# Three of eight low parts of each next expert's weights made by GpSimd instead of VectorE, in a decoder layer with a mixture of experts

## The chip, the cores and the metric

The kernel runs on one core of a Trainium2 chip. The metric is the device time of one execution in microseconds (us). Before the change three runs gave 993.51, 994.58 and 995.72 us, median 994.58.

## The reference

One decoder layer over 32 sequences of 128 tokens with 256 channels, all in fp32, with a layer norm after each of three parts:

```python
x = layernorm(x + retention(x, past_kv, W_qkv, gn_weight, gn_bias))     # 16 heads of 16
x = layernorm(x + cross_attention(x, ctx, Wq, Wk, Wv, Wo, bo))          # causal, 16 heads
x = layernorm(x + moe(x, router_w, w_fc, b_fc, w_proj, b_proj))

# moe: 4096 tokens, 8 experts, 256 -> 1024 -> 256, the two best experts of each token
probs = softmax(xf @ router_w.T); topk_probs, topk_idx = top_k(probs, 2)
combine = topk_probs / sum(topk_probs), scattered to [tokens, 8]
h = gelu_new(einsum('nc,ech->neh', xf, w_fc) + b_fc)
y = einsum('nec,ne->nc', einsum('neh,ehc->nec', h, w_proj) + b_proj, combine)
```

Only the third part is touched here. The kernel computes an expert only for the tokens that are sent to it.

## The kernel before, in words

The attention part runs sequence by sequence until about 540 us. While it runs, GpSimd (POOL) sends each token's row to a region of its two experts in device memory. From about 510 to 960 us come the experts (their first slot is mixed with the last sequences). The rows of an expert are worked off in slots of 256 rows. Four early slots of expert 0 come first, then `expert` runs for each of the eight experts over its own slots (a loop whose count is read from a table).

The matmuls need more than one pass of the reduced fp32 format (fp32r), so every operand is split into a high part (rounded to fp32r) and a low part (the original minus the high part). Within a slot there are eight steps j, one for each 128 of the 1024 hidden channels:

- PE (TensorE): `fc(j)`, six matmuls into a bank (line 820), and three steps later `proj(j-3)`, four matmuls (lines 834 and 836), which read the hidden values' high and low parts. In step 5 it also transposes the next slot's rows (line 801).
- ACT (ScalarE): `hidden` makes the high part of gelu (line 1155) and its full value `h_f` (line 1161). The second waits for the low part of two steps before (`h_split`), since `h_f` has two buffers. After step 7, `xs_high` makes the next slot's `xs_hi` (line 1148).
- DVE (VectorE): `hidden_low` subtracts, `h_lo = h_f - h_hi` (line 1490), which releases `proj(j)`. After j = 0 it weights the slot before (lines 1529, 1532), which releases POOL's scatter-adds. After j = 7 it makes `xs_lo` (line 1460), which lets PE start the next slot, and after that adds the biases (lines 1516, 1521).
- POOL (GpSimd): `add`, two indirect DMAs a slot that add the weighted rows to `residual_sum` (line 1714).

An expert's weights are loaded into `w_raw` by the SP queue and split into eight pieces of 128x512. This is done in the first slot of the expert before it, so in seven first slots: ACT makes the high parts 0 to 6 behind each `hidden` (`split_hi`, line 1075), DVE high part 7 (`last_hi`, line 1380), and DVE all low parts behind each `hidden_low` (`split_lo`, line 1385). Each low part waits for its high part (`raw_hi`) and counts in `w_ready`; after the last one DVE waits until all eight are counted, and then lets SP load new weights. Expert 0's own weights are split in the attention part, where POOL makes the low parts (`first_low`, line 1746).

All five queues run in written order, and are tied only by semaphores: an instruction that waits holds up all that stands behind it on its engine.

Of the kernel before, what the change touches and what calls it, by code (L numbers as in the profile page):

```python
# [16 lines left out]
HC = H // P  # L17
# [13 lines left out]
DRAIN_IDLE = 3  # L31
EARLY = 4
EARLY_SEQ = 27
MOST = 2 * N_TOK // SLOT + E + EARLY
BITS = 10 * P + 2 * TW
SMALL = 2 * P + 33
# [27 lines left out]
def decoder_kernel(nc, x, turned, kv_blocks, w_qkv, gn_scale, gn_shift, wq_t, wk_t, wv_t, wo_t, bo,  # L64
                   router_t, w_fc, b_fc, w_proj, b_proj, decay_c, small_c, bits_c, out):
    f32, f32r, bf16 = mybir.dt.float32, mybir.dt.float32r, mybir.dt.bfloat16
    i32, u32 = mybir.dt.int32, mybir.dt.uint32
    ALU, ACT, AX = mybir.AluOpType, mybir.ActivationFunctionType, mybir.AxisListType
# [3 lines left out]
    with ctx:  # L72
        def sb(name, shape, dt=f32):
            return ctx.enter_context(nc.sbuf_tensor(name, shape, dt))
# [7 lines left out]
        def sem(name):  # L82
            return ctx.enter_context(nc.semaphore(name))
# [20 lines left out]
        w_raw = sb("w_raw", [P, WROW])  # L104
# [132 lines left out]
        w_hi, w_lo = ([w[:, i, :] for w in w_both] for i in range(2))  # L237
# [46 lines left out]
        s = {k: sem(k) for k in names}  # L284
# [66 lines left out]
        def _(sp):  # L351
# [44 lines left out]
            def early_rows(g):  # L396

                if g:
                    sp.wait_ge(s["rows_turned"], g + EVER)
                    sp.wait_ge(s["meta_ready"], g + EVER)  # L400
                    apart(sp)
                sp.dma_start(rows[:, :, :],
                             sent_flat[g * SLOT:(g + 1) * SLOT, :].rearrange("(h p) c -> p h c", p=P))\
                    .then_inc(s_rows, 16)

            def step(k):
# [5 lines left out]
                if k == B - 1:  # L412
                    for r in range(4):
                        sp.wait_ge(s_sent[r], 32 * len(range(r, EARLY_SEQ, 4)))
                    early_rows(0)
# [57 lines left out]

            n_all = sp.value_load(tab_i[0:1, 3, 0:1], min_val=E + EARLY, max_val=MOST)
            sp.wait_ge(s["rows_turned"], n_all + EVER)
# [9 lines left out]
            out_rows = out.rearrange("b t c -> (b t) c")  # L485
            n_add = sp.value_load(tab_i[0:1, 3, 1:2], min_val=16 * (E + EARLY), max_val=16 * MOST)
            for half in range(HALVES):
# [471 lines left out]
        def _(act):  # L959
# [19 lines left out]
            def w_high(i):  # L979

                hi, _, raw, loaded, n = parts[i]
                act.wait_ge(s[loaded], n)
                A(hi, raw, ACT.Copy).then_inc(s["w_high"], 1)
# [258 lines left out]
        def _(dve):  # L1242
            V = nc.vector

            def w_low(i):

                hi, lo, raw, _, _ = parts[i]
                dve.wait_ge(s["w_high"], i + 1)
                V.tensor_tensor(lo, raw, hi.bitcast(f32), ALU.subtract).then_inc(s["w_split"], 1)
# [111 lines left out]
            def put(c):  # L1361
# [9 lines left out]
                dve.sem_inc(s["placed"], 1)  # L1371
                if c.n == EARLY_SEQ - 1:
                    V.tensor_scalar(filled[:, 0:1], filled[:, 0:1], float(EARLY * SLOT), None, ALU.max)

            PIECE = WROW // HC

            def last_hi(e, par):
                at = slice((HC - 1) * PIECE, HC * PIECE)
                dve.wait_ge(s["raw_hi"], HC * (e + 1) - 1)
                V.tensor_copy(w_hi[par][:, at], w_raw[:, at]).then_inc(s["raw_hi"], 1)  # L1380

            def split_lo(e, par, j):
                at = slice(j * PIECE, (j + 1) * PIECE)
                dve.wait_ge(s["raw_hi"], HC * e + j + 1)
                last = V.tensor_tensor(w_lo[par][:, at], w_raw[:, at], w_hi[par][:, at].bitcast(f32),
                                       ALU.subtract)
                last.then_inc(s["w_ready"], 1)
                if j == HC - 1:
                    dve.wait_ge(s["w_ready"], HC * (e + 1))
                    dve.sem_inc(s["raw_split"], 1)  # L1390
# [67 lines left out]
            def split_rows(g):  # L1458
                dve.wait_ge(s["xs_chain"], g + 1)
                V.tensor_tensor(xs_lo[:, :, :].rearrange("p k t -> p (k t)"), ps_xs(g)[:, :],  # L1460
                                xs_hi[:, :, :].bitcast(f32).rearrange("p k t -> p (k t)"), ALU.subtract)\
                    .then_inc(s["xs_ready"], 1)
# [22 lines left out]
            def hidden_low(g, j):  # L1485

                dve.wait_ge(s["h_done"], HC * g + j + 1 + EVER)
                if j >= 4:
                    dve.wait_ge(s["y_done"], HC * g + j - 3)
                V.tensor_tensor(h_lo[j % 4][:, :], h_f[j % 2][:, :], h_hi[j % 4][:, :].bitcast(f32),  # L1490
                                ALU.subtract).then_inc(s["h_split"], 1)

            def slot(g, e, split_to=None, beside=None):
                for j in range(HC):
                    hidden_low(g, j)
                    if j == 0:
                        gate_rows(g - 1)
                    if j == HC - 1:
                        split_rows(g + 1)
                    if split_to and j == HC - 1:  # L1500
                        last_hi(*split_to)
                    if split_to:
                        split_lo(*split_to, j)
                    if beside:
                        beside(j)
                add_rows(g, e)

            def add_rows(g, e):

                dve.wait_ge(s["meta_ready"], g + 1 + EVER)  # L1510
                V.tensor_copy(meta[:, :, :], meta_next[:, :, :]).then_inc(s["y_chain"], 1)
                dve.wait_ge(s["y_chain"], g + 1)
                take_rows(g + 1)
                dve.wait_ge(s["y_done"], HC * (g + 1))
                for half in range(HALVES):
                    V.tensor_tensor(y_b[:, half, :], ps_out(g, half), bproj(e), ALU.add)\
                        .then_inc(s["y_biased" if not two_sums(g) else "y_first"], 1)
                if two_sums(g):
                    for half in range(HALVES):
                        dve.wait_ge(s["y_first"], HALVES * (g - 2) + half + 1)  # L1520
                        V.tensor_tensor(y_b[:, half, :], ps_sum[half][:, C:2 * C], y_b[:, half, :], ALU.add)\
                            .then_inc(s["y_biased"], 1)

            def gate_rows(g):

                for half in range(HALVES):
                    dve.wait_ge(s_added[half], 16 * (g + EVER))
                    apart(dve)
                V.tensor_copy(meta_i[:, :], meta[:, :, 1])
                dve.wait_ge(s["y_biased"], HALVES * (g + 1) + EVER)  # L1530
                for half in range(HALVES):
                    V.tensor_scalar(y_w[:, half, :], y_b[:, half, :], meta[:, half, 0:1], None, ALU.mult)\  # L1532
                        .then_inc(s["y_weighted"], 1)
# [71 lines left out]
            dve.wait_ge(s["consts_expert"], 16 * CONSTS_EXPERT)  # L1605
            drain()
            slot(1, 0, None, last_norms)
            slot(2, 0, None, last_places)
            for g in range(3, EARLY - 1):
                slot(g, 0)  # L1610
# [44 lines left out]
        def _(pool):  # L1655
            G = nc.gpsimd
# [50 lines left out]
            def add(g, before):  # L1707
                for half in range(HALVES):

                    pool.wait_ge(s["y_weighted"], HALVES * g + half + 1)  # L1710
                    apart(pool)
                    pool.wait_ge(s_added[1 - half], 16 * (before + EVER))
                    apart(pool)
                    G.indirect_dma_start(total, bass.IndirectOffsetOnAxis(meta_i[:, half:half + 1], 0),  # L1714
                                         y_w[:, half, :], None, compute_op=ALU.add)\
                        .then_inc(s_added[half], 16)

            def drain():
# [8 lines left out]
                for r in range(4):  # L1727
                    pool.wait_ge(s_total[r], 16 * len(range(r, EARLY_SEQ, 4)))
                add(0, 0)
# [9 lines left out]

            PIECE = WROW // HC  # L1740

            def first_low(j):

                at = slice(j * PIECE, (j + 1) * PIECE)
                pool.wait_ge(s["raw_hi"], j + 1)
                G.tensor_tensor(w_lo[0][:, at], w_raw[:, at], w_hi[0][:, at].bitcast(f32), ALU.subtract)\
                    .then_inc(s["w_ready"], 1)
                if j == HC - 1:
                    pool.wait_ge(s["w_ready"], HC)
                    pool.sem_inc(s["raw_split"], 1)  # L1750
# [35 lines left out]
                pool.wait_ge(s_total[r], 16 * (B // 4))  # L1786

            def expert(e, par, n_slots, before, has_next, has_after):
                with pool.Fori(0, n_slots) as i:
                    add(before + i, before)  # L1790

# [91 lines left out]
```

## Time and profile before

| | |
|---|---|
| median of 3 runs | 994.58 us (993.51 to 995.72) |
| the profiled execution's own time | 990.76 us |
| its span | 988.7 us |
| mean granted TensorE clock | 0.978 |
| busy: PE, PEld (weight load), DVE, ACT, POOL | 924.2, 822.0, 664.0, 605.2, 385.0 us |
| low part of a piece on DVE, line 1385 | 56 times, mean 692 ns |
| `h_lo` on DVE, line 1490 | 288 times, mean 426 ns |
| scatter-add on POOL, line 1714 | 72 times, mean 1624 ns |

The profile is of one execution. Its own time lies 2.1 us over its span and 3.8 us under the median of the runs. Times in the timelines are microseconds from the start of the span. A duration in a row reaches from the start of an instruction to its last write, and the next one can begin before that: two subtractions of 128x512 and 128x256 on DVE overlap by 0.08 us. Line numbers are those of the kernel before.

### The profile page before, as it was taken

To read this page: it belongs to the slowest core of one execution; us is meant where nothing else is said; L and a number is where in the kernel's file an instruction comes from. 1 tells how busy PE (TensorE), PEld (TensorE's weight loads), DVE (VectorE), ACT (ScalarE), POOL (GpSimd) and SP (SyncE) were. 2 spreads that over 40 slices of the span, in tenths; PEclk is the share of its full clock that TensorE was granted. 3 is DMA by queue.
4 is the path that set the end of the run, shared out by engine and by line. 5 is a ranking of instruction groups with operands and counts; after the bars stand their busy time and mean duration, and the time that the engine had idled before them with its cause. 6 is when DMAs were issued, how large, how long until landed. Compare 5 with 4: busy or idle time off the path is not lost.

```text
span 988.7 us, 29856 instructions
## 1 busy us (share of the span) xinstructions
PE 924.2 (93%) x10845; PEld 822.0 (83%) x10845; DVE 664.0 (67%) x1977; ACT 605.2 (61%) x1528; POOL 385.0 (39%) x639
## 2 busy tenths in 40 slices
PE   5899999999999999999888999999999999999950
PEld 4788888888888888888667899999999999999950
DVE  3577777777877877877734677575755775665536
ACT  4556656656556666666446567565755765665536
POOL 0324555555544656664523522222222323232223
PEclk9999999999999999999989999999999999999985
DMA  8111141112111111122112453523435343533228
GB/s 279 50 34 56 61 142 45 56 55 66 56 49 45 62 56 61 55 64 85 44 30 44 119 130 58 138 44 53 129 53 139 79 103 53 129 48 46 45 37 336
DMA packets 57362, 79.91 MB, mean 81 GB/s; under 512 B 5728, under 2 KB 46048, under 8 KB 57120
## 3 DMA queue, kind: packets, MB, share of 16 engines
q1 hardware_dynamic: 41504, 58.50, 18.5%
q0 software_dynamic: 13536, 18.16, 10.8%
q10 hardware_dynamic: 2208, 1.73, 0.6%
q8 instruction: 71, 1.16, 0.5%
q14 instruction: 43, 0.35, 0.1%
HBM read 52.10 MB, written 29.71 MB: 83 GB/s over the span
## 4 chain that ended last, share of the span: by engine, by line
PE 79%; ACT 6%; DVE 5%; issue 4%; DMA 2%; SPq 1%; POOL 1%; ACTq 0%; DVEq 0%; POOLq 0%
PE bank L820 16%; PE bank L834 11%; PE bank L511 11%; PE bank L836 5%; PE bank L647 4%; PE bank L673 4%; PE bank L718 3%; PE bank L573 3%; PE bank L626 3%; PE bank L694 3%; PE bank L598 3%; PE bank L593 2%; ACT h_f L1161 2%; PE bank L732 2%; ACT last_out L1237 1%
## 5 line engine op out<-in xcount | busy, mean ns | idle before, releaser
L820 PE MATMUL bank<-xs_hi,w_both 128*128 128x256 f32 x1152 | 241.6, 287 | 0.0
L1155 ACT ACTIVATE h_parts<-bank,bfc_s 128x256 fp32r<-128x256 f32 x288 | 140.0, 486 | 155.3 <-PE bank L820 150.6
L1714 POOL DMA_INDIRECT residual_sum<-y_w,meta_i x72 | 116.9, 1624 | 300.4 <-DVE y_w L1532 267.0
L1490 DVE TENSOR_TENSOR h_parts<-h_f,h_parts 128x256 fp32r<-128x256 f32 x288 | 121.5, 426 | 143.9 <-ACT h_f L1161 138.4
L834 PE MATMUL bank<-w_both,h_parts 128*128 128x512 f32 x544 | 200.0, 398 | 1.1 <-DVE h_parts L1490 1.1
L820 PEld LDWEIGHTS bank<-xs_hi,w_both 128*128 128x128 f32 x1152 | 191.0, 190 | 7.8 <-issue 1.7
L820 PE MATMUL bank<-xs_lo,w_both 128*128 128x256 f32 x576 | 162.7, 282 | 0.0
L836 PE MATMUL bank<-w_both,h_parts 128*128 128x256 f32 x544 | 153.0, 281 | 0.0
L1161 ACT ACTIVATE h_f<-bank,bfc_s 128x256 f32<-128x256 f32 x288 | 139.4, 484 | 3.9 <-DVE h_parts L1490 3.4
L834 PEld LDWEIGHTS bank<-w_both,h_parts 128*128 128x128 f32 x544 | 102.5, 188 | 19.9 <-DVE h_parts L1490 3.5
L820 PEld LDWEIGHTS bank<-xs_lo,w_both 128*128 128x128 f32 x576 | 109.4, 190 | 0.1
L836 PEld LDWEIGHTS bank<-w_both,h_parts 128*128 128x128 f32 x544 | 102.7, 189 | 0.0
L1267 DVE TENSOR_REDUCE row_max<-bank 128x4 f32<-128x512 f32 x128 | 79.4, 682 | 6.9 <-PE bank L651 6.9
L1262 DVE TENSOR_TENSOR ret_p<-bank,decay 128x512 f32<-128x512 f32 x128 | 79.3, 682 | 1.6 <-PE bank L573 1.6
L1049 ACT ACTIVATE att_p<-bank 128x512 f32<-128x512 f32 x128 | 66.1, 603 | 22.0 <-PE bank L682 21.9
L1704 POOL DMA_INDIRECT sent_rows<-x_row,pos x64 | 64.2, 1003 | 22.2 <-issue 14.5
L673 PE MATMUL bank<-qx_own,kxT 32*128 32x256 f32 x512 | 45.0, 405 | 0.0
L647 PE MATMUL bank<-kxT,qx_own 32*128 32x128 f32 x1024 | 44.9, 287 | 0.0
L511 PE MATMUL bank<-h_parts,wqk_hi 128*128 128x256 f32 x128 | 39.2, 306 | 4.7 <-DVE xc_lo L1254 4.0
L647 PEld LDWEIGHTS bank<-kxT,qx_own 32*128 32x128 f32 x1024 | 36.2, 185 | 5.9 <-issue 3.0
L511 PE MATMUL bank<-wv_hi,h_parts 128*128 128x256 f32 x128 | 38.8, 303 | 2.2 <-ACT q_own L1001 2.0
L1013 ACT ACTIVATE v_ret<-bank 128x256 f32<-128x256 f32 x32 | 12.3, 384 | 46.5 <-PE bank L511 46.5
(184 smaller groups left out, 2139.7 us busy)
## 6 DMA issues: line engine op xcount, KB each, us to landing
rows<-sent_rows SPq DMA_DIRECT2D x37, 258.0 KB
xc_raw<-in_turned SPq DMA_DIRECT2D x32, 256.0 KB, 3.0
w_raw<-in_w_fc SPq DMA_DIRECT2D x8, 1024.0 KB
w_raw<-in_w_proj SPq DMA_DIRECT2D x8, 1024.0 KB
x_t<-in_x SPq DMA_DIRECT2D x32, 128.0 KB, 2.2
residual_sum<-x_row SPq DMA_DIRECT2D x32, 128.0 KB, 1.7
last_in<-residual_sum SPq DMA_DIRECT2D x7, 512.0 KB, 7.3
result<-last_out SPq DMA_DIRECT2D x7, 512.0 KB, 2.7
```

Of the source, the lines that this page charges most:

```text
L511: last = mm(to, left, right, start=(n == 0), stop=(n == len(passes) - 1))
L647: mm(ps_s[r][:, at], qx_own[c.r % 2][tile(r), k, j, :], kxT[c.n // 2 % 2][tile(r), k, c.n % 2 * T:(c.n % 2 + 1) * T], start=(k == 0 and j ...
L673: mm(ps_s[r][:, at], kxT[c.n // 2 % 2][tile(r), k, c.n % 2 * T:(c.n % 2 + 1) * T], qx_own[c.r % 2][tile(r), k, :, :].rearrange("p j t -> p ...
L820: last = mm(ps_h(g, j), w[:, at:at + P], v[:, k, :], start=(n == 0), stop=(n == 3 * NCH - 1))
L834: mm(ps_sum[half][:, :], h_hi[j % 4][:, cols], w[:, :, at:at + C], start=(j == 0), stop=False)
L836: last = mm(to, h_lo[j % 4][:, cols], w[:, 0, at:at + C], start=False, stop=(j == HC - 1))
L1155: A(h_hi[j % 4][:, :], ps_h(g, j), ACT.Gelu_apprx_tanh, bias=bias)
L1161: A(h_f[j % 2][:, :], ps_h(g, j), ACT.Gelu_apprx_tanh, bias=bias)\
L1262: V.tensor_tensor(ret_p[:, r, :], ps_s[r][:, :], decay[:, r, :], ALU.mult)\
L1267: V.reduce_max(row_max[:, r, 0:HPT], ps_s[r][:, :].rearrange("p (h s) -> p h s", s=T), AX.X)\
L1490: V.tensor_tensor(h_lo[j % 4][:, :], h_f[j % 2][:, :], h_hi[j % 4][:, :].bitcast(f32), ALU.subtract).then_inc(s["h_split"], 1)
L1714: G.indirect_dma_start(total, bass.IndirectOffsetOnAxis(meta_i[:, half:half + 1], 0), y_w[:, half, :], None, compute_op=ALU.add)\
```

## The change

In every first slot that has a next expert, the low parts 0, 1 and 2 of the next expert's weights are taken out of DVE's order and put into POOL's, ahead of the loop of scatter-adds of the present expert. The operands, the semaphores and their counts stay the same. POOL's scatter-adds of the last slot of the expert before still stand in front of the three low parts, since they belong to that expert's loop.

```diff
+ON_POOL = (0, 1, 2)
...
@@ vector, slot()
-                    if split_to:
+                    if split_to and j not in ON_POOL:
                         split_lo(*split_to, j)
...
@@ gpsimd
+            def split_lo(e, par, j):
+
+                at = slice(j * PIECE, (j + 1) * PIECE)
+                pool.wait_ge(s["raw_hi"], HC * e + j + 1)
+                G.tensor_tensor(w_lo[par][:, at], w_raw[:, at], w_hi[par][:, at].bitcast(f32), ALU.subtract)\
+                    .then_inc(s["w_ready"], 1)
...
             def expert(e, par, n_slots, before, has_next, has_after):
+                if has_next:
+                    for j in ON_POOL:
+                        split_lo(e + 1, 1 - par, j)
                 with pool.Fori(0, n_slots) as i:
                     add(before + i, before)
```

POOL's queue before, from the scatter-adds of one expert's loop to those of the next (`w_both` holds a weight piece's high and low parts; the branches are the loop's):

```order
L1714 DMA residual_sum<-y_w,meta_i 4352x256
L1710 REGISTER_ALU
L1714 DMA residual_sum<-y_w,meta_i 4352x256
L1789 REGISTER_ALU
L1789 COMPARE_AND_BRANCH
L1789 UNCONDITIONAL_BRANCH
L1789 ISA
L1712 ISA
L1714 DMA residual_sum<-y_w,meta_i 4352x256
```

The same place after the change (line numbers are 1 to 11 higher):

```order
L1715 DMA residual_sum<-y_w,meta_i 4352x256
L1711 REGISTER_ALU
L1715 DMA residual_sum<-y_w,meta_i 4352x256
L1800 REGISTER_ALU
L1800 COMPARE_AND_BRANCH
L1747 TENSOR_TENSOR w_both<-w_raw,w_both 128x512 x3
L1800 UNCONDITIONAL_BRANCH
L1800 ISA
L1713 ISA
L1715 DMA residual_sum<-y_w,meta_i 4352x256
```

Three subtractions now stand between the last pair of one expert and the first pair of the next.

DVE's queue before, steps 1 to 3 of a first slot (`h_parts` is the hidden values' high and low parts):

```order
L1532 TENSOR_SCALAR y_w<-y_b,meta 128x256 x2
L1385 TENSOR_TENSOR w_both<-w_raw,w_both 128x512
L1487 REGISTER_ALU
L1490 TENSOR_TENSOR h_parts<-h_f,h_parts 128x256
L1385 TENSOR_TENSOR w_both<-w_raw,w_both 128x512
L1487 REGISTER_ALU
L1490 TENSOR_TENSOR h_parts<-h_f,h_parts 128x256
L1385 TENSOR_TENSOR w_both<-w_raw,w_both 128x512
L1487 REGISTER_ALU
L1490 TENSOR_TENSOR h_parts<-h_f,h_parts 128x256
L1385 TENSOR_TENSOR w_both<-w_raw,w_both 128x512
```

And after:

```order
L1533 TENSOR_SCALAR y_w<-y_b,meta 128x256 x2
L1488 REGISTER_ALU
L1491 TENSOR_TENSOR h_parts<-h_f,h_parts 128x256
L1488 REGISTER_ALU
L1491 TENSOR_TENSOR h_parts<-h_f,h_parts 128x256
L1488 REGISTER_ALU
L1491 TENSOR_TENSOR h_parts<-h_f,h_parts 128x256
L1386 TENSOR_TENSOR w_both<-w_raw,w_both 128x512
```

Steps 3 to 7 of DVE, and the queues of PE, ACT and SP, keep their order.

## Rows read from the trace of the kernel before

**Rows 1.** The page, part 1: busy us of each engine, share, instructions.
```profile
PE 924.2 (93%) x10845; PEld 822.0 (83%) x10845; DVE 664.0 (67%) x1977; ACT 605.2 (61%) x1528; POOL 385.0 (39%) x639
```

**Rows 2.** Stretches: length, busy PE, PEld, DVE, ACT, POOL, granted clock, DMA.
```profile
597.45:608.00 10.55, 10.55 (x74) 9.58 (x74) 9.71 (x21) 9.34 (x23) 3.28 (x2) 1.00 0.30 43
610.00:622.00 12.00, 11.83 (x84) 10.90 (x83) 6.76 (x21) 6.85 (x17) 3.10 (x2) 1.00 0.33 55
```

**Rows 3.** Waits from 560 to 960 us: waiter, releaser, total us, times, longest.
```profile
DVE h_parts L1490 <- ACT h_f L1161: 124.6, 155, 1.7
...
PEld bank L834 <- DVE h_parts L1490: 3.5, 11, 0.4
...
PEld bank L820 <- issue: 1.3, 7, 0.2
```

**Rows 4.** Timeline, PEld, second expert: start, us, engine, line, [idle before].
```profile
606.82 0.19 PEld L834 LDWEIGHTS bank<-w_both,h_parts 128*128 128x128 f32 x1
...
607.64 0.19 PEld L820 LDWEIGHTS bank<-xs_hi,w_both 128*128 128x128 f32 x1 [0.18 <-issue]
...
610.94 0.19 PEld L834 LDWEIGHTS bank<-w_both,h_parts 128*128 128x128 f32 x1 [0.37 <-DVE h_parts L1490]
```

**Rows 5.** Timeline, ACT, first slot of the second expert.
```profile
597.45 0.63 ACT L1075 ACTIVATE w_both<-w_raw 128x512 fp32r<-128x512 f32 x1
...
598.68 0.65 ACT L1075 ACTIVATE w_both<-w_raw 128x512 fp32r<-128x512 f32 x1
...
605.74 0.57 ACT L1161 ACTIVATE h_f<-bank,bfc_s 128x256 f32<-128x256 f32 x1
```

**Rows 6.** Timeline, DVE, beginning of the same slot.
```profile
598.59 0.68 DVE L1385 TENSOR_TENSOR w_both<-w_raw,w_both 128x512 fp32r<-128x512 f32 x1
599.19 0.42 DVE L1490 TENSOR_TENSOR h_parts<-h_f,h_parts 128x256 fp32r<-128x256 f32 x1
599.53 0.68 DVE L1385 TENSOR_TENSOR w_both<-w_raw,w_both 128x512 fp32r<-128x512 f32 x1
```

**Rows 7.** Timeline, DVE, its second half.
```profile
603.11 0.69 DVE L1385 TENSOR_TENSOR w_both<-w_raw,w_both 128x512 fp32r<-128x512 f32 x1
...
606.34 0.43 DVE L1490 TENSOR_TENSOR h_parts<-h_f,h_parts 128x256 fp32r<-128x256 f32 x1
...
607.43 0.42 DVE L1380 CAST w_both<-w_raw 128x512 fp32r<-128x512 f32 x1
...
608.73 0.17 DVE L1511 COPY meta<-meta_next 128x4 f32<-128x4 f32 x1 [0.16 <-DVE w_both L1385]
```

**Rows 8.** Timeline, POOL, the same slot.
```profile
599.29 1.73 POOL L1714 DMA_INDIRECT residual_sum<-y_w,meta_i  x1 [7.94 <-DVE y_w L1532]
601.33 1.55 POOL L1714 DMA_INDIRECT residual_sum<-y_w,meta_i  x1 [0.31 <-issue]
```

**Rows 9.** Line 1746, POOL: count, ns min/median/max, first and last start.
```profile
L1746 POOL TENSOR_TENSOR w_both<-w_raw,w_both x8: 1278/1284/1287, 330.6 to 435.0; 128x512 fp32r<-128x512 f32 x8
```

**Rows 10.** Timeline, POOL, one of these low parts.
```profile
344.97 1.28 POOL L1746 TENSOR_TENSOR w_both<-w_raw,w_both 128x512 fp32r<-128x512 f32 x1
```

**Rows 11.** Timeline, DVE, beside it.
```profile
343.57 1.88 DVE L1262 TENSOR_TENSOR ret_p<-bank,decay 128x512 f32<-128x512 f32 x3
345.37 1.45 DVE L1254 TENSOR_TENSOR xc_lo<-xc_raw,h_parts 128x512 fp32r<-128x512 f32 x1
```

**Rows 12.** Line 1254, DVE: count, ns min/median/max.
```profile
L1254 DVE TENSOR_TENSOR xc_lo<-xc_raw,h_parts x32: 680/684/1452, 8.4 to 452.5; 128x512 fp32r<-128x512 f32 x32
```

**Rows 13.** Timeline, POOL, two small operations.
```profile
556.00 0.28 POOL L1682 TENSOR_TENSOR x_row<-gap_e,x_row 128x1 f32<-128x1 f32 x1
556.24 0.38 POOL L1683 TENSOR_TENSOR x_row<-tok,small 128x1 f32<-128x1 f32 x1
```

**Rows 14.** Timeline, DVE, beside them.
```profile
555.81 0.76 DVE L1490 TENSOR_TENSOR h_parts<-h_f,h_parts 128x256 fp32r<-128x256 f32 x2
```

**Rows 15.** A stretch with a PE gap of 2.80 us, columns as in rows 2.
```profile
524.00:530.00 6.00, 3.38 (x50) 3.07 (x52) 2.96 (x13) 5.08 (x9) 3.21 (x9) 1.00 0.30 82
```

## The prediction

> **What bounds the kernel now.** I read the busy times first, then stretches of the expert part, then the waits, and last the timelines of one first slot. PE is the bound: 924.2 of 988.7 us [rows 1]. The 10.55 us of a first slot are all PE, and so are 11.83 of 12.00 us in the slot behind it, at full clock; DVE and ACT are also near full in the first slot (9.71 and 9.34 us) and have room in the second (6.76 and 6.85) [rows 2]. Seven slots are such first slots, so the reader should ask what little PE loses there. In the whole expert part PE's weight loads wait 3.5 us for `h_lo` in 11 places and 1.3 us in 7 places for the next slot's `xs_lo` (shown as "issue") [rows 3]. The second expert shows where: no wait at the last `proj` at 606.82, 0.18 us at the first `fc` of the next slot, 0.37 us at its first `proj` [rows 4]. So the slack is used up at the end of a first slot: what is late there for `h_lo` of step 7 comes out of PE one for one.
>
> Who makes it late? ACT's period in the first slot is 1.23 us a step (597.45 to 598.68, two gelus and a high part) [rows 5]. DVE's work of a step is 0.60 + 0.34 = 0.94 us (598.59 to 599.19 for the low part, then to 599.53 for `h_lo`) [rows 6]. At step 7 ACT's `h_f` starts at 605.74 and lasts 0.57, to 606.31 [rows 5], and DVE's `h_lo` starts at 606.34 [rows 7]. DVE goes at ACT's pace there; it does not hold PE.
>
> **The change, part by part.** *Removed:* 3 low parts in 7 slots, 21 x 0.60 = 12.6 us of DVE's order. They lie in steps 0 to 2, at 598.59 to about 601 [rows 6]. Nothing behind them gets earlier at the slot's end, because from step 2 on DVE follows ACT again, and PE's waits stand behind step 7 [rows 4]. I value the removal at 0. All waits of [rows 3] on `h_lo` and `xs_lo` together, 4.8 us, would be its upper bound; its lower bound is 0, as less work in order can't delay DVE by itself.
>
> *Added:* 21 low parts on POOL at 1.284 us each [rows 9], 27 us. POOL has the time: its engine is busy 385.0 us [rows 1]. They stand behind the scatter-adds of the last slot of the expert before. That pair starts at 599.29, when DVE has weighted the rows, and ends at 601.33 + 1.55 = 602.88; the first add is long, 1.73 against 1.55, and may shorten to that when DVE's low parts beside it are gone [rows 8]. With 0.31 us between queue entries, as between the two adds, POOL's first low part can start at 599.29 + 1.55 + 0.31 + 1.55 + 0.31 = 603.0. All its high parts are long made. So the lows run in steps 4 to 7, the part in which PE's slack runs out, not in steps 0 to 2 from which they were taken.
>
> *What they meet there.* The trace has four low parts of POOL that a DVE subtraction with both operands in SBUF fell on. At 344.97 POOL begins, for 1.28 us [rows 10]; at 345.37 DVE begins `xc_lo`, of the same size, and takes 1.45 us instead of 0.684 [rows 11, 12]. It ends at 346.82, 0.57 behind POOL's end at 346.25. The pattern stands four times in the trace, with 1.44 or 1.45 us each, at the four of the eight low parts that met such a subtraction. The `ret_p` products beside the same low part, one of whose operands is a PSUM bank, keep their pace: 1.88 us for three [rows 11]. So DVE's two-SBUF-operand instructions stand still until POOL is done reading; DVE loses 346.82 - 0.684 - 344.97 = 1.17 us from POOL's start. The other way round, POOL's small operations at 556.00 and 556.24 stretch while DVE makes two `h_lo` back to back, and the first of them finishes between the two [rows 13, 14]: the two engines take turns.
>
> The Trainium skill states the same ("SBUF — State Buffer", Who interferes with whom): a VectorE instruction with two SBUF inputs and a GpSimd instruction that reads SBUF exclude each other, and the later one waits for the whole instruction of the first. By that rule a low part holds DVE 1.28 us, by the rows 1.17 us. The trace agrees with the rule but for this 0.11 us, and its consequence speaks against the change; the sum below takes both as ends.
>
> *The sum in one first slot.* `h_lo` (h_f and h_parts) and `split_lo` (w_raw and w_both) both read twice from SBUF. From 603.0 until `h_lo` of step 7, the shared access has to carry POOL's three low parts, 3 x 1.17 = 3.51 to 3 x 1.28 = 3.84 us, and DVE's low 4, h5, low 5, h6, low 6: 3 x 0.60 + 2 x 0.34 = 2.48 us. `h_lo` of step 7 then starts at 603.0 + 2.48 + 3.51 = 608.99 to 609.32, not 606.34 [rows 7]: 2.65 to 2.98 us late. Whether POOL comes first, the turns alternate, or POOL goes three times in a row, the sum of the work is the same. ACT's step 7 waits for `h_lo` 5, but that is done by about 607 in each order, before it matters. PE's slack at that point is 0, so PE loses the same. Behind it the tail (`xs_lo`, high part 7, low part 7, biases) is DVE's as before, with POOL finished, and the 0.37 us wait of the next slot stays. I take 2.85 us, nearer to the end that adds a handover.
>
> *Total:* 7 x 2.85 = 20.0 us. On the profiled execution, 990.76 + 20.0 = 1010.8. That execution lies 3.8 us under the median of the runs; on the median, 994.58 + 20.0 = 1014.6. The ends 2.65 and 2.98 give 1013.1 to 1015.4. If the adds stay long, POOL starts about 0.2 to 1 us later, which costs up to 0.3 us more a slot: 1017.5.
>
> *No cost:* the longer way of `w_ready`: POOL's last low part ends near 608.7, before DVE's own low part 7, which moves from before 608.73 [rows 7] to past 611. The new load of weights starts later by the same 2.85 us as the slot that needs it. The next scatter-add comes a slot later. PE's gaps: in the stretch with a gap of 2.80 us the granted clock stayed 1.00 [rows 15], so I charge nothing for a fallen clock, though mine are as long.
>
> **The rivals.**
> *DVE keeps the access while it has a backlog.* POOL's first low part delays low 4 by 603.0 + 1.17 - 603.11 = 1.06 us; DVE then runs low 4, h5, low 5, h6, low 6 in 2.48 us and starts step 7 at 606.65, 0.3 late. POOL's second and third fall in the tail: high part 7, a copy at 607.43, may wait too, and the wait for `w_ready` becomes the bound, with POOL's last part ending at about 606.65 + 0.34 + 2 x 1.28 = 609.6 and DVE's `meta` copy at 609.8 instead of 608.73 [rows 7]. That is 1.1 to 1.5 us a slot, 7 x 1.3 = 9.1: 1003.7. For it: back-to-back instructions may keep hold of it. Against: the small POOL operation that got in between two `h_lo` [rows 13, 14].
>
> *No exclusion that counts, so no slower.* The mechanism would be that POOL works its low parts beside DVE at 1.28 us each. They are done by 603.0 + 3.84 = 606.8, 2 us before `w_ready` is wanted; PE loses nothing, and DVE's lag at step 1 is gone. Gain 0 to 1 us: 993.6 to 994.6. It decides if the delay of a DVE low part beside POOL's is under some 0.1 us. Against it stand four delays of 0.76 us; for it only that those are `xc_lo`, and no expert slot has shown it.
>
> *More than counted:* the clock falls in the gaps. At the half level each microsecond of PE work takes one more; if two microseconds of work behind each gap ran so, 7 x 2 = 14 us more, 1029. For it: several gaps close behind one another; against: [rows 15].
>
> **How the numbers follow.** Exclusion with turns 0.68, a backlog that keeps DVE going (or something between the two) 0.21, no exclusion that counts 0.06, more than counted 0.05. The predicted time is that of the first, 1014.6. The low end goes to the second case, 1002.5, the high end to 1019.5 for long adds and dearer handovers; what is left out is the third and fourth case and the edges. A measurement can tell about 0.2% (2 us) from no change. The third case splits into 0.02 faster and 0.04 same; the others are all slower, with 0.94.
>
> **What would show it.** Right: three subtractions of about 1.3 us on POOL in each first slot, starting 5.5 us behind the first high part; beside them `h_lo` and `split_lo` of up to 1.6 us; a wait of PE for `h_lo` of 2 to 3 us at the end of each first slot; seven of these, and every other slot as before. Wrong: `h_lo` of 0.43 us beside POOL's low parts; or POOL's low parts themselves stretched to 3 us with PE's wait moved behind `meta` (the second case); or low parts that start before step 3.

## The result, and the profile after

The changed kernel took 1018.61 us (median of 4 runs, 1014.83 to 1020.75) against 995.02 us for the kernel before (4 runs). The two medians differ by 23.6 us. The ratio is 1.025 with a 95% interval of 1.0228 to 1.0272, so 2.5% slower: 24.8 us of the 993 us that the kernel before took in the later runs (medians 992.96 to 993.85). The forecast was 20.0 us slower, with a range up to 1019.5 us. The median lies just inside it; 1.025 times the 995.02 us of the kernel before gives 1019.9 us and lies just outside. The sign and the exclusion of DVE by POOL held. The size was short by a fifth, DVE and POOL took no turns, and PE waited mostly in the middle of the slot, not at its end.

The page of the profile after, busy times as in [rows 1], and three groups of part 5 (line, engine, operation, busy time, mean ns, idle time before and what ended it). Line numbers on DVE and PE are one higher than before:

```profile
PE 938.9 (92%) x10845; PEld 832.5 (82%) x10845; DVE 678.6 (67%) x1956; ACT 605.3 (59%) x1528; POOL 405.9 (40%) x660
...
L835 PE MATMUL bank<-w_both,h_parts 128*128 128x512 f32 x544 | 205.9, 407 | 18.8 <-DVE h_parts L1491 18.5
...
L835 PEld LDWEIGHTS bank<-w_both,h_parts 128*128 128x128 f32 x544 | 104.3, 192 | 41.9 <-DVE h_parts L1491 25.6
...
L1386 DVE TENSOR_TENSOR w_both<-w_raw,w_both 128x512 fp32r<-128x512 f32 x35 | 55.5, 1587 | 0.9
```

DVE makes 21 low parts fewer and is busy 14.6 us longer. Its 35 low parts average 1587 ns instead of 692. PE's weight loads wait 25.6 us for `h_lo` where they waited 3.5 [rows 3]; its matmuls stood idle 18.5 us for it.

All uses of DVE's low-part line and of POOL's new one (count, ns min/median/max, first and last start):

```profile
L1386 DVE TENSOR_TENSOR w_both<-w_raw,w_both x35: 677/681/5233, 581.6 to 898.7; 128x512 fp32r<-128x512 f32 x35
```

```profile
L1747 POOL TENSOR_TENSOR w_both<-w_raw,w_both x21: 1812/1855/1887, 581.8 to 892.2; 128x512 fp32r<-128x512 f32 x21
```

The median of DVE's low parts is as before and the longest is 5233 ns: there is one such in each of the seven first slots. The timelines of the third expert's first slot show it. First DVE, then POOL, then PE's weight loads:

```profile
659.51 0.43 DVE L1491 TENSOR_TENSOR h_parts<-h_f,h_parts 128x256 fp32r<-128x256 f32 x1 [0.82 <-ACT h_f L1162]
660.03 5.22 DVE L1386 TENSOR_TENSOR w_both<-w_raw,w_both 128x512 fp32r<-128x512 f32 x1
665.17 0.41 DVE L1491 TENSOR_TENSOR h_parts<-h_f,h_parts 128x256 fp32r<-128x256 f32 x1
665.51 0.68 DVE L1386 TENSOR_TENSOR w_both<-w_raw,w_both 128x512 fp32r<-128x512 f32 x1
...
667.98 0.42 DVE L1491 TENSOR_TENSOR h_parts<-h_f,h_parts 128x256 fp32r<-128x256 f32 x1
```

```profile
659.37 1.55 POOL L1715 DMA_INDIRECT residual_sum<-y_w,meta_i  x1 [0.30 <-issue]
...
660.38 4.31 POOL L1747 TENSOR_TENSOR w_both<-w_raw,w_both 128x512 fp32r<-128x512 f32 x3
```

```profile
665.64 0.19 PEld L835 LDWEIGHTS bank<-w_both,h_parts 128*128 128x128 f32 x1 [2.89 <-DVE h_parts L1491]
666.58 0.19 PEld L835 LDWEIGHTS bank<-w_both,h_parts 128*128 128x128 f32 x1 [0.29 <-DVE h_parts L1491]
...
668.45 0.19 PEld L835 LDWEIGHTS bank<-w_both,h_parts 128*128 128x128 f32 x1 [0.29 <-DVE h_parts L1491]
```

POOL's three low parts run in one burst from 660.38 to 664.69. DVE's low part 3 begins 0.35 us ahead of them and ends at 665.25, 0.56 us behind them. No turns are taken. After that DVE goes at its own 0.94 us a step, and PE's weight loads wait for it four times, 3.76 us together: 2.89 us at `proj(4)` and three times 0.29 behind it.

To price a slot without the noise of the rest, I take from each trace the time from the first high part of the first such slot to that of the seventh (ACT, line 1075 before, 1076 after). Six first slots lie in it. It is 573.39 to 860.30 before, 286.91 us, and 577.15 to 884.96 after, 307.81 us: 20.90 / 6 = 3.48 us a slot, 24.4 us for seven. The 3.8 us by which the first of these slots starts later lie in the attention part, which is not touched; the profiled execution after is also the slowest of its four, at the lowest mean granted clock (0.962; the others had 0.968 to 0.972).

The granted clock has a part in it. The matmuls that end PE's gap in two first slots after the change, the third and the fourth:

```profile
665.64 0.50 PE L835 MATMUL bank<-w_both,h_parts 128*128 128x512 f32 x1 [2.69 <-DVE h_parts L1491]
...
728.33 0.50 PE L835 MATMUL bank<-w_both,h_parts 128*128 128x512 f32 x1 [2.59 <-DVE h_parts L1491]
```

Stretches of the same two slots (length, busy times of PE, PEld, DVE, ACT, POOL, granted clock, DMA):

```profile
665.00:667.00 2.00, 1.36 (x6) 0.98 (x7) 2.00 (x5) 1.29 (x4) 0.00 (x0) 1.00 0.00 0
667.00:669.00 2.00, 2.00 (x11) 1.33 (x10) 2.00 (x6) 0.92 (x3) 0.00 (x0) 1.00 0.00 0
...
728.00:730.00 2.00, 1.68 (x7) 1.24 (x8) 2.00 (x5) 1.61 (x5) 0.00 (x0) 0.87 0.04 8
730.00:732.00 2.00, 2.00 (x8) 1.71 (x8) 2.00 (x5) 0.61 (x2) 0.00 (x0) 0.50 0.01 4
732.00:734.00 2.00, 2.00 (x14) 1.81 (x13) 1.68 (x7) 0.00 (x0) 0.00 (x0) 0.77 0.00 0
```

In the third slot PE had no matmul for 2.69 us and went on at 2.4 GHz. In the fourth it had none for 2.59 us, and the clock fell to 1.2 GHz about a microsecond after it had work again. The clock fell in three of the seven slots, with gaps of 2.59, 2.60 and 2.68 us; in the four others the gaps were 2.53, 2.59, 2.69 and 2.69. So the length of the gap did not decide it, and what did stays open. Their excess over before is 4.01 and 3.81 us (the third of them is the last, which the measure does not hold), that of the four others is 3.20, 3.25, 3.31 and 3.32, mean 3.27. So in this execution the shut-out itself costs 7 x 3.27 = 22.9 us and the clock some 3 x 0.6 = 1.8 us, together 24.7. That this comes so near to the 24.8 of the runs is partly chance: their interval is 2 us wide on either side, and no trace shows how often the clock fell in the other executions.

### The profile page after: what moved, and what is told of

The parts are those of the page before. It is cut to its first block, busy times and chain, and to the rows that moved or that the text cites. A ratio compares the mean times of both kernels' runs of the same rounds, so it can differ in the third digit from the quotient of the medians.

```text
span 1017.7 us, 29856 instructions
## 1 busy us (share of the span) xinstructions
PE 938.9 (92%) x10845; PEld 832.5 (82%) x10845; DVE 678.6 (67%) x1956; ACT 605.3 (59%) x1528; POOL 405.9 (40%) x660
## 4 chain that ended last, share of the span: by engine, by line
PE 80%; issue 6%; DVE 5%; ACT 5%; DMA 1%; POOL 1%; DVEq 0%; ACTq 0%; SPq 0%; POOLq 0%
PE bank L821 16%; PE bank L512 11%; PE bank L835 11%; PE bank L837 6%; PE bank L648 4%; PE bank L674 4%; PE bank L574 3%; PE bank L695 3%; PE bank L719 3%; PE bank L627 3%; PE bank L599 3%; PE bank L594 2%; ACT h_f L1162 2%; PE bank L733 2%; ACT last_out L1238 1%
## 5 line engine op out<-in xcount | busy, mean ns | idle before, releaser
L1715 POOL DMA_INDIRECT residual_sum<-y_w,meta_i x72 | 112.0, 1556 | 303.9 <-DVE y_w L1533 280.0
L835 PE MATMUL bank<-w_both,h_parts 128*128 128x512 f32 x544 | 205.9, 407 | 18.8 <-DVE h_parts L1491 18.5
L835 PEld LDWEIGHTS bank<-w_both,h_parts 128*128 128x128 f32 x544 | 104.3, 192 | 41.9 <-DVE h_parts L1491 25.6
L837 PEld LDWEIGHTS bank<-w_both,h_parts 128*128 128x128 f32 x544 | 104.8, 193 | 0.0
L1386 DVE TENSOR_TENSOR w_both<-w_raw,w_both 128x512 fp32r<-128x512 f32 x35 | 55.5, 1587 | 0.9
L1670 POOL TENSOR_TENSOR gmsq<-gm 128x1 f32<-128x1 f32 x32 | 6.2, 193 | 89.1 <-DVE gm L1284 89.1
```

The source lines that it names most:

```text
L835: mm(ps_sum[half][:, :], h_hi[j % 4][:, cols], w[:, :, at:at + C], start=(j == 0), stop=False)
L837: last = mm(to, h_lo[j % 4][:, cols], w[:, 0, at:at + C], start=False, stop=(j == HC - 1))
```

## The experiments

The excess a slot is measured as above in each run's trace; "clock" is the number of the seven first slots in which the granted clock fell. Microseconds in the text below are the ratio less 1, times 993 us.

| kernel | ratio to before, 95% interval | excess a slot, us | clock |
|---|---|---|---|
| the change (3 low parts in a burst) | 1.0250 (1.0228, 1.0272) | 3.48 | 3 |
| one low part | 1.0072 (1.0055, 1.0089) | 0.87 | 0 |
| two low parts | 1.0152 (1.0135, 1.0169) | 2.13 | 0 |
| turns | 1.0242 (1.0216, 1.0269) | 3.04 | 1 |
| three subtractions extra | 1.0284 (1.0266, 1.0302) | 3.98 | 6 |
| three fills extra | 1.0006 (0.9994, 1.0017) | -0.01 | 0 |
| three copies extra | 1.0228 (1.0206, 1.0249) | 2.97 | 3 |
| three low parts early | 1.0050 (1.0035, 1.0065) | 0.82 | 0 |
| low part 7 | 0.9996 (0.9984, 1.0008) | -0.04 | 0 |
| low part 7, later | 0.9988 (0.9977, 0.9999) | -0.39 | 0 |

**One and two low parts.** How the price grows with the burst.

```diff
-ON_POOL = (0, 1, 2)
+ON_POOL = (0,)        # and (0, 1)
```

> GpSimd makes one low part (0) instead of three, DVE seven. Theory (a burst of GpSimd subtractions shuts DVE's two-SBUF-operand instructions out until it ends, then DVE needs 0.94 us a step from there): the burst is 1.9 us instead of 4.3, DVE's low part 3 takes about 2.7 us, h_lo of step 7 is about 1.0 us late, and the kernel is 7 x 1.0 = 7 us slower than before. Rival (a fixed price for waking GpSimd in that place, whatever it makes there): 15 to 24 us slower, as with three. Rival (price in proportion to the parts): 8 us.

> GpSimd makes two low parts (0 and 1). Theory: burst 3.1 us, h_lo of step 7 about 2.2 us late, 7 x 2.2 = 15.5 us slower than before. Fixed price: 24 us. Proportion: 16 us.

Measured 7.1 and 15.1 us. A fixed price is out. The longest low part of DVE is 2806 ns with one and 4040 ns with two, so each part of the burst adds 1.2 us to the shut-out. The theory's 7 and 15.5 us hit, but the price in proportion (8 and 16 us) lies inside the intervals too. The traces lean to the theory: the first part costs 0.87 us a slot, the second 1.26 and the third, where the clock stayed up, 1.14.

**Turns.** POOL's low part j waits until `h_lo` of step 3 + j is done.

```diff
                 pool.wait_ge(s["raw_hi"], HC * e + j + 1)
+                pool.wait_ge(s["h_split"], HC * before + 4 + j + EVER)
```

> The three low parts stay on GpSimd, but each waits for one more h_lo of DVE (of steps 3, 4 and 5), so that DVE gets in between them. Theory that the access is one resource and only the sum of the work on it counts, in whatever order: the same 22 to 25 us slower as with the burst; DVE's low parts 3, 4 and 5 take 1.8 to 2.5 us each instead of one of 5.2. Rival (a long burst is what costs, since DVE also loses the work it could have done between): 10 to 16 us slower.

Timelines of DVE and of POOL in the third expert's first slot:

```profile
659.15 2.80 DVE L1386 TENSOR_TENSOR w_both<-w_raw,w_both 128x512 fp32r<-128x512 f32 x1
661.87 0.41 DVE L1491 TENSOR_TENSOR h_parts<-h_f,h_parts 128x256 fp32r<-128x256 f32 x1
662.21 0.68 DVE L1386 TENSOR_TENSOR w_both<-w_raw,w_both 128x512 fp32r<-128x512 f32 x1
662.81 1.50 DVE L1491 TENSOR_TENSOR h_parts<-h_f,h_parts 128x256 fp32r<-128x256 f32 x1
```

```profile
659.51 1.88 POOL L1748 TENSOR_TENSOR w_both<-w_raw,w_both 128x512 fp32r<-128x512 f32 x1
662.37 1.66 POOL L1748 TENSOR_TENSOR w_both<-w_raw,w_both 128x512 fp32r<-128x512 f32 x1 [0.97 <-DVE h_parts L1491]
```

The price is that of the burst within the intervals, and the 10 to 16 us of the rival are out: it is mostly the sum of the work on the shared access that decides, and not its order. In the traces the turns are a little cheaper, 2.98 to 3.05 us in four slots without a fallen clock against 3.27. The second low part of POOL comes 0.16 us behind DVE's low part 4 and is stretched itself, to 1.66 us, and then `h_lo` takes 1.50. I had expected DVE's low parts to be hit each time; from the second turn on it is `h_lo`.

In the first of the seven slots not even low part 3 was hit. DVE, then POOL:

```profile
581.83 0.69 DVE L1386 TENSOR_TENSOR w_both<-w_raw,w_both 128x512 fp32r<-128x512 f32 x1
582.56 1.69 DVE L1491 TENSOR_TENSOR h_parts<-h_f,h_parts 128x256 fp32r<-128x256 f32 x1
```

```profile
582.08 1.87 POOL L1748 TENSOR_TENSOR w_both<-w_raw,w_both 128x512 fp32r<-128x512 f32 x1
```

DVE's low part 3 began 0.25 us ahead of POOL's subtraction, just as in the first of these slots after the change. There it took 5.12 us, here 0.69, and `h_lo` of step 4 was shut out instead. The excess of this slot is 2.33 us.

**Extra work on POOL beside all eight low parts on DVE.** Three subtractions of 128x512 that read bias values, or three fills of 128x1024, or three copies of 128x1024, each into spare tiles and in the place of the change (shortened: `spare`, `bias_a`, `bias_b` and `bias` stand for slices of tiles, and a wait for POOL's own burst before is left out).

```diff
+                if has_next:
+                    for j in range(3):
+                        pool.wait_ge(s["raw_hi"], HC * (e + 1) + j + 1)
+                        G.tensor_tensor(spare[:, 0:512], bias_a, bias_b, ALU.subtract)
+                        # or G.memset(spare, 0.0), or G.tensor_copy(spare, bias)
```

> DVE makes all eight low parts as before, and GpSimd makes three subtractions of the same size in the same place, on data that nobody else touches, into a spare tile. Theory (the access to SBUF is what is shared, and taking parts 0 to 2 off DVE was worth nothing): as slow as with the change, 23 to 26 us over before, DVE's low part 3 takes about 5.2 us. Rival (the delay comes from the same weight tiles or their semaphores): within 1 us of before. Rival (the relief of DVE was worth its 12.6 us): 35 us slower.

> DVE makes all eight low parts, and GpSimd fills three spare tiles of 128x1024 with zeros in the place of the three subtractions, so it writes SBUF but reads none. Theory (DVE's second operand and GpSimd's reads share one access): within 1 us of before, DVE's low parts at 0.69 us beside the fills; a copy in DVE's faster mode could wait once. Rival (any work of GpSimd on SBUF shuts DVE out): some 2 to 4 us a slot, 14 to 25 us slower.

> DVE makes all eight low parts, and GpSimd makes three copies of 128x1024 into spare tiles in the place of the three subtractions: it reads SBUF with one operand and writes it. Theory that any GpSimd instruction that reads SBUF shuts DVE's two-SBUF-operand instructions out: DVE's low part 3 takes about as long as the burst of copies (3 to 4.5 us), 14 to 25 us slower than before. Rival (only GpSimd instructions with two SBUF operands do): within 1 us of before, as with the fills.

The subtractions cost 28.2 us though they touch neither the weight tiles nor `w_ready`. (The bias values that they read are read by DVE too, but only in its additions behind step 7.) That rules out the weight tiles and their count. The fills cost nothing: they start 0.89 us apart and last 3.3 us together, from 4.9 to 8.2 us behind the first high part in the second slot, and DVE's 56 low parts stay at 680 to 695 ns. The copies last 3.6 us together and cost 22.7 us, with low parts of up to 4573 ns. So it is POOL's reading from SBUF, with one operand or two, that shuts out a DVE instruction which reads two.

The difference between the extra subtractions and the change is what parts 0 to 2 were worth on DVE. It is 28.2 - 24.8 = 3.4 us, but the clock fell in six slots instead of three. The one slot of the six without a fall has an excess of 3.44 us against a mean of 3.27, some 0.2 us, 1 us in all; one slot is too few to say more. In this run the scatter-adds were also longer, as in the kernel before (1.66 us for the first against 1.54 after the change), so the burst started 0.12 us later. In its first slot they took 2.37 and 2.07 us, the burst started 1.31 us later than after the change, and the excess was 4.52 us with a fallen clock.

**Early.** The three low parts go in front of the scatter-adds of the last slot of the expert before.

```diff
-                for g in range(2, EARLY):
+                for g in range(2, EARLY - 1):
                     add(g, 0)
...
                         split_lo(e + 1, 1 - par, j)
                 with pool.Fori(0, n_slots) as i:
-                    add(before + i, before)
+                    add(before - 1 + i, before - 1)
...
-            experts(expert, slots)
+            n_all = experts(expert, slots)
+            add(n_all - 1, n_all - 1)
```

> The three low parts stand in front of the scatter-adds of the last slot of the expert before, so they run in steps 0 to 2 as their high parts come, about 1.24 us apart. Theory: DVE's h_lo of steps 1 and 2 are shut out until about 4.4 us behind the first high part unless a gap of GpSimd lets them in; ACT's step 3 waits for h_lo of step 1 and is up to 1.9 us late; 5 to 14 us slower than before, less than the change. Rival (DVE's slack in steps 0 to 2 takes it all): within 2 us of before.

5.0 us, the lower end of the theory. DVE's timeline (third expert), then POOL's second and third low part:

```profile
651.44 1.66 DVE L1533 TENSOR_SCALAR y_w<-y_b,meta 128x256 f32<-128x256 f32 x2
...
653.01 1.49 DVE L1491 TENSOR_TENSOR h_parts<-h_f,h_parts 128x256 fp32r<-128x256 f32 x1
...
654.43 1.51 DVE L1491 TENSOR_TENSOR h_parts<-h_f,h_parts 128x256 fp32r<-128x256 f32 x1
```

```profile
652.90 1.32 POOL L1747 TENSOR_TENSOR w_both<-w_raw,w_both 128x512 fp32r<-128x512 f32 x1
...
654.18 1.47 POOL L1747 TENSOR_TENSOR w_both<-w_raw,w_both 128x512 fp32r<-128x512 f32 x1
```

The weighting of the rows, a multiplication with one tensor operand, is shut out too: 1.66 us for two instead of 0.61 before. And here the engines do take turns. `h_lo` of step 1 begins at 653.01, while POOL's second part runs, and ends at 654.50, while the third runs; that one is stretched to 1.47 us, and `h_lo` of step 2 ends 0.29 us behind it. It is so in all seven slots. So three low parts close behind one another shut DVE out as a whole where they stand ready behind a scatter-add, and one at a time where each follows its high part. No `h_lo` takes longer than 1.51 us, and PE waits once in the slot, 1.25 us. The price is a quarter, 0.82 us against 3.27. How much of that is owed to the turns and how much to the slack that PE still has in these steps was not separated.

**Low part 7, then later.** POOL makes the last low part instead of the first three, in DVE's tail, in which DVE adds biases to PSUM banks. POOL also takes over the wait for `w_ready` and the release of `w_raw` from DVE. The second version waits in addition for DVE's copy of the next meta.

```diff
-ON_POOL = (0, 1, 2)
+ON_POOL = (7,)
...
                 pool.wait_ge(s["raw_hi"], HC * e + j + 1)
+                pool.wait_ge(s["meta_ready"], before + 2 + EVER)      # later version
                 G.tensor_tensor(w_lo[par][:, at], ...).then_inc(s["w_ready"], 1)
+                pool.wait_ge(s["w_ready"], HC * (e + 1))
+                pool.sem_inc(s["raw_split"], 1)
```

> GpSimd makes low part 7 alone, behind DVE's high part 7, and gives the weights' buffer free itself; DVE makes parts 0 to 6. DVE's tail (meta, biases, h_lo of the next slot's step 0) has no two-SBUF-operand instruction of note while it runs. Theory: DVE's tail is 0.7 us shorter, PE's wait of 0.37 us at the next slot's first proj goes, 7 x 0.35 = 2.5 us faster than before (0.25%). Rival (another instruction of the tail is shut out as well, or PE waits for the accumulator anyway): no change within 1 us.

> As low7, but GpSimd's low part 7 also waits until DVE has copied the next slot's meta (line 1457, the 128x4 copy that took 1.19 us instead of 0.17 beside low part 7 in the run before). Then DVE has only additions with a PSUM operand until h_lo of the next slot. Theory: the copy takes 0.17 us again, h_lo of step 0 of the next slot starts 12.2 us behind the first high part instead of 13.0, PE's 0.37 us wait there goes, 7 x 0.35 = 2.5 us faster than before (ratio 0.9975). Rival (h_lo of step 0 falls on the end of low part 7, or another wait takes over): within 1 us.

The first version gained nothing, because a copy of 128x4 fell on POOL's subtraction. POOL, then DVE:

```profile
659.42 1.28 POOL L1747 TENSOR_TENSOR w_both<-w_raw,w_both 128x512 fp32r<-128x512 f32 x1 [5.06 <-DVE w_both L1381]
```

```profile
659.25 0.16 DVE L1512 COPY meta<-meta_next 128x4 f32<-128x4 f32 x1
659.54 1.19 DVE L1457 COPY meta_next<-rows 128x4 f32<-128x4 f32 x1
```

The second version keeps it clear, POOL's subtraction first, then DVE:

```profile
658.20 1.28 POOL L1748 TENSOR_TENSOR w_both<-w_raw,w_both 128x512 fp32r<-128x512 f32 x1 [4.34 <-DVE meta_next L1457]
```

```profile
657.94 0.17 DVE L1457 COPY meta_next<-rows 128x4 f32<-128x4 f32 x1
658.05 0.76 DVE L1517 TENSOR_TENSOR y_b<-bank,bproj_rest 128x256 f32<-128x256 f32 x2
658.72 0.75 DVE L1522 TENSOR_TENSOR y_b<-bank,y_b 128x256 f32<-128x256 f32 x2
659.52 0.43 DVE L1491 TENSOR_TENSOR h_parts<-h_f,h_parts 128x256 fp32r<-128x256 f32 x1
```

`h_lo` of the next slot starts 659.52 - 647.33 = 12.2 us behind the first high part, as expected, and PE's wait of 0.37 us [rows 4] is gone. The trace gives 0.39 us a slot, 2.7 us. The ratio is 0.9988 with an interval of 0.9977 to 0.9999: 1.2 us faster, so the sign is just clear of 1, and the 2.5 us of the expectation (0.9975) lie just outside the interval. It is the only version that beats the kernel before, and its interval overlaps that of the first version, so the runs alone don't tell the two apart; their traces do, 0.39 us a slot against 0.04. The gain is not the subtraction's alone, since DVE lost its wait for `w_ready` (0.16 us in [rows 7]) as well.

## Why the prediction was right or wrong

*PE's slack is used up at the end of a first slot.* Right in size: `h_lo` of step 7 came 3.47 us late, and PE lost 3.27. One low part already costs 0.87 us a slot. But PE did not wait at the end alone: 2.89 us of the 3.76 fell on `proj(4)`, in the middle of the slot, because low part 3 held up `h_lo` of step 4.

*The removal is worth 0.* Right to about 1 us of 12.6, as far as one slot can tell: three subtractions extra cost 3.44 us in a slot without a fallen clock, the change 3.27.

*POOL's reads and DVE's two-operand reads exclude each other.* Right, by the subtractions, the copies and the fills. The rival without exclusion is out.

*The sum in one first slot.* This is the step that failed: it was mis-sized, 2.85 us instead of 3.27 without the clock, for `h_lo` of step 7 that started 3.47 us late instead of 2.65 to 2.98. Three sizes in it were off, and two of them cancel. I let POOL start 0.31 us behind the recorded end of the second scatter-add, 5.55 us behind the first high part; it starts 1.01 us behind that add's start, at 4.77 us, 0.78 earlier. So low part 3 and `h_lo` of step 4 were still to do as well: from the burst's end at 9.08 us DVE works until it starts `h_lo` of step 7 at 12.37 (667.98 in the timeline), 3.29 us instead of 2.48, 0.81 more. What is left is the burst. It lasts 4.31 us, not 3.51 to 3.84, which is 0.47 to 0.80 more. Its starts are 1.25 us apart, but each part is recorded with about 1.86 us, so the first seems to begin 0.57 us too early, inside the record of the scatter-add; in that time DVE's low part 3 made no headway either. The sum took the shared access to be at work without a pause, and there it was not: DVE's low part 3 and POOL's three, 0.68 + 3 x 1.28 = 4.52 us by their times alone, took 5.22 us.

*Turns.* Wrong in this place: POOL's burst behind the scatter-add is not interrupted, and a low part of DVE takes 5.2 us, not the 1.6 that was to show the forecast right. The engines can take turns, as the two small operations of [rows 13] suggested and the early low parts show. It cost the sum little, as turns, when forced, cost 3.0 us a slot against 3.27. The rival "DVE keeps the access while it has a backlog" is out, and so is its 9 us.

*A gap leaves the clock alone.* Wrong in three of seven slots. [rows 15] showed a gap of 2.80 us with the clock at 1.00, and one such row was too little to set this at zero: its 2.80 us are a wait of the weight loads, 2.62 us without a matmul, and gaps of 2.53 to 2.69 us went both ways after the change. It is 1.8 us of the 4.8 that were missing in the profiled execution, at a far lower price than the 2 us a slot of the rival.

The rule of the Trainium skill ("SBUF — State Buffer", Who interferes with whom) that I weighed holds in its operands: two SBUF inputs on one side, a read on the other. Its other half, that who issues first gets the access for the whole instruction, does not fit here by the recorded starts: DVE's low part 3 was first by 0.25 to 0.35 us in all seven slots and still ended behind POOL's burst. In the first slot of the run with turns, with the same 0.25 us, it ran undisturbed. Where POOL's subtraction did not directly follow a scatter-add (second turn above), the trace agrees with the rule.

## What to carry to other kernels

Work taken off a busy engine is worth what that engine makes others wait for at that place, and here it was next to nothing. Before giving GpSimd work that reads SBUF, list the VectorE instructions beside it: those with two SBUF operands, and plain copies and scalings, stood still here for as long as it lasted. Put it beside VectorE instructions that read PSUM, and hold it back by a semaphore until they come; one subtraction then gained 0.1%, at the edge of what the runs can tell, where one in the middle of the slot cost 0.7%.

## What the runs showed of the hardware that I had not expected

- A row of GpSimd subtractions behind an indirect DMA is not interrupted: one subtraction of DVE took up to 5233 ns beside three of them, and 4.6 us beside three copies. A row whose parts each came just behind their high parts let DVE in after each: no `h_lo` over 1.51 us.
- A 128x4 copy on DVE took 1.19 us beside a GpSimd subtraction instead of 0.17, and two scalings of 128x256 took 1.66 instead of 0.61.
- A GpSimd subtraction right behind an indirect DMA starts about 0.54 us before that DMA's recorded end (660.38 against 660.92). DVE's low part, begun 0.35 us earlier, then had all its 0.56 us still to do when the burst was over. Why it had done nothing in its head start, and why it got through in one slot of the run with turns, stays open: beside a scatter-add alone DVE's low parts kept to 0.69 us, one of 0.77 apart.
